# Queries, keys, values and gate of a head group as one product of seven half-size products

## The reference

```
q, k, v = xn @ Wq.T, xn @ Wk.T, xn @ Wv.T          # 32 query heads, 8 key/value heads of 128
q, k = rmsnorm(q) * q_norm_w, rmsnorm(k) * k_norm_w
a = softmax(q k^T / sqrt(128) + slope[h] * (key - query), causal) @ v
s = a @ Wo.T
g = silu(xn @ W.T + bias + sum_n 2 lora_weights[n] * (xn @ A_n.T) @ B_n.T)
x + s * g
```

## Time and profile before

| | us |
|---|---|
| median of 3 runs (2854.84 to 2856.85) | 2855.52 |
| the profiled execution | 2851.0 |
| its span, first to last instruction | 2849.2 |
| PE busy, weight loads busy | 2763.9, 2516.4 |
| DVE, ACT, POOL busy | 2198.6, 1259.9, 1136.4 |
| q1, the queue of SP | 237.35 MB, 25.2% of the engines' time |

### The profile page before, as it was taken

The page is one execution under the profiler, slowest core; times in us unless marked ns, Lnnn a source line. Parts: engine busy times, 40 slices in busy tenths (PEclk is TensorE's granted clock), DMA queues, the critical chain, the costliest instruction groups (busy, mean ns, idle before and its releaser), DMA issues.

```text
span 2849.2 us, 47788 instructions
## 1 busy us (share of the span) xinstructions
PE 2763.9 (97%) x18256; PEld 2516.4 (88%) x18256; DVE 2198.6 (77%) x5317; ACT 1259.9 (44%) x2907; POOL 1136.4 (40%) x555
## 2 busy tenths in 40 slices
PE   7999999998999999999899999999989999999997
PEld 6899999997889999999688999999878999999985
DVE  6877777778787777777878777777787877777788
ACT  3444444444344444444434444444443444444443
POOL 3334334333434434334353334443344433344334
PEclk9999999999999999999999999999999999999999
DMA  7222222212422221221341222222224222222213
GB/s 256 97 79 67 65 70 64 64 61 96 168 66 86 75 67 60 68 75 57 106 168 52 72 75 75 67 69 65 71 96 160 67 61 66 75 75 68 74 62 113
DMA packets 80659, 240.40 MB, mean 84 GB/s; under 512 B 9008, under 2 KB 17328, under 8 KB 79920
## 3 DMA queue, kind: packets, MB, share of 16 engines
q1 hardware_dynamic: 80432, 237.35, 25.2%
HBM read 217.39 MB, written 19.92 MB: 83 GB/s over the span
## 4 chain that ended last, share of the span: by engine, by line
PE 83%; DVE 14%; issue 2%; ACT 0%; DMA 0%; SPq 0%; POOL 0%; POOLq 0%; DVEq 0%; ACTq 0%
PE proj L402 20%; PE proj L403 20%; PE proj L404 20%; PE tr L472 4%; PE sc L402 3%; PE ot L403 3%; PE ot L404 3%; PE sc L404 3%; PE sc L403 3%; DVE g_buf L1155 3%; PE ot L402 3%; PE tr L484 2%; DVE sq L1060 2%; DVE prob L1126 1%; DVE xtok L1050 1%
## 5 line engine op out<-in xcount | busy, mean ns | idle before, releaser
L916 POOL TENSOR_TENSOR wb_lo<-stage_b,wb_hi 128x1024 fp32r<-128x1024 f32 x158 | 382.3, 2419 | 1424.6 <-ACT wb_hi L684 1424.6
L402 PE MATMUL proj<-wa_hi,xn_hi 128*128 128x256 f32 x3072 | 878.3, 286 | 0.9 <-issue 0.9
L404 PE MATMUL proj<-wa_hi,xn_lo 128*128 128x256 f32 x3072 | 869.3, 283 | 0.0
L403 PE MATMUL proj<-wa_lo,xn_hi 128*128 128x256 f32 x3072 | 869.2, 283 | 0.0
L402 PEld LDWEIGHTS proj<-wa_hi,xn_hi 128*128 128x128 f32 x3072 | 589.0, 192 | 2.5 <-issue 2.1
L403 PEld LDWEIGHTS proj<-wa_lo,xn_hi 128*128 128x128 f32 x3072 | 589.3, 192 | 0.3
L404 PEld LDWEIGHTS proj<-wa_hi,xn_lo 128*128 128x128 f32 x3072 | 588.9, 192 | 0.0
L911 POOL TENSOR_TENSOR wa_lo<-stage_a,wa_hi 128x1024 fp32r<-128x1024 f32 x192 | 463.1, 2433 | 228.7 <-ACT wa_hi L670 228.7
L709 ACT ACTIVATE prob<-prob,negmax 128x128 f32<-128x128 f32 (+3 forms) x512 | 286.5, 560 | 431.0 <-DVE negmax L1116 430.1
L402 PE MATMUL proj<-o_hi,wb_hi 128*128 128x512 f32 x1024 | 431.5, 421 | 41.7 <-DVE acc L1143 40.3
L1143 DVE TENSOR_TENSOR acc<-acc,proj 128x512 f32<-128x512 f32 x480 | 326.9, 682 | 116.0 <-PE proj L404 113.3
(11 more groups left out here) (120 smaller groups left out, 4778.9 us busy)
## 6 DMA issues: line engine op xcount, KB each, us to landing
stage_a<-wa SPq DMA_DIRECT2D x196, 512.0 KB, 3.6
stage_b<-wo SPq DMA_DIRECT2D x128, 512.0 KB, 3.7
stage_b<-weff SPq DMA_DIRECT2D x30, 512.0 KB, 3.8
xtok<-x_tok SPq DMA_DIRECT2D x4, 2048.0 KB, 8.6
outT<-acc SPq DMA_DIRECT2D x32, 256.0 KB, 2.0
gate_dram<-x_buf SPq DMA_DIRECT2D x28, 256.0 KB, 2.2
xtok<-xT SPq DMA_DIRECT2D x16, 256.0 KB, 4.1
xtok<-gate_dram SPq DMA_DIRECT2D x16, 256.0 KB, 4.7
```

Of the source, the lines that this page charges most:

```text
L402: pe.matmul(out, hi_l, hi_r, start=first, stop=False)
L403: pe.matmul(out, hi_l, lo_r, start=False, stop=False)
L404: return pe.matmul(out, lo_l, hi_r, start=False, stop=last)
L916: pool.tensor_tensor(wb_lo[:, slot, :], stage_b[:, slot, :], wb_hi[:, slot, :], ALU.subtract).then_inc(wb_ready, 1)
```

## The change

The 512 tokens by 1024 of xn are seen as 2x2 blocks (token halves, width halves), and the 1024x896 weights of a group (q0, q1, k, half the gate, then q2, q3, v, the other half of the gate) as 2x2 blocks of 512x448. Their product is made with seven products of half size (Strassen's scheme in Winograd's form) instead of eight: P1 and P2 of plain blocks, P6, P7, P4, P5, P3 with one or both sides a sum of blocks.

- **Weight sums.** For each of 8 groups, once, the seven 512x448 operands are made and stored to DRAM (`wu`, two halves each): three plain blocks by `store_halves`, four sums by `store_sums`, after `weight_sums` on VectorE (half 0) and GpSimd (half 1). Group 0's and 1's are made in the opening, group n+2's during group n (n = 0 to 5). Wo is copied once from DRAM to DRAM (`copy_b`) and loaded from there.
- **Token sums.** `x_sum` makes four of them in place on GpSimd; seven operands of 4 chunks are turned and split in 14 fills a batch, spread over steps (6,3) to (7,2).
- **Pieces.** `piece(n, p, t)`: 128 of the half's 256 tokens, 4 chunks, three matmuls of 448 columns each. P2, P7 and P3 go on in the bank that holds P1, P6 and P5, after that has been read. `UNIT` puts P1, P2 into step 0, P6, P7 into 1, P4 into 2, P5, P3 into 3 of the group before. ScalarE copies P1 and P1+P2 out; VectorE adds the others to rows of `raw` (`take_piece`), ten a group.
- **Gate.** Its 128 columns of group n come out with the group's rows, are turned (four transposes), and finished in the same group; there is no gate product of its own.
- **Uniform groups.** All 32 groups are the same code written out, with constants in place of registers; the pieces of the next batch's group 0 are made in group 7, and each batch's result is finished in steps 1 and 2 of the next batch's group 0, in two halves that share four slots of `xtok`.
- **Squares** are taken by ScalarE with an accumulator (`squares`, 20 a group), the value's low half by GpSimd. Weights are loaded into the buffer of their low part and split there; there are four half slots.

```
-KV, Q01, Q23 = 0, 1, 2
-
-PROJ = [[(Q23, t) for t in range(4)],
-        [(KV, 0), (KV, 1), (KV, 2)],
-        [(KV, 3), (Q01, 0), (Q01, 1)],
-        [(Q01, 2), (Q01, 3)]]
...
+HALF = 448
...
+NP = 7
+HW = 2 * NP
+P1, P2, P6, P7, P4, P5, P3 = range(NP)
+UNIT = [(P1, P2), (P6, P7), (P4,), (P5, P3)]
+FRESH = (P1, P6, P4, P5)
+CHAINED = {P2: P1, P7: P6, P3: P5}
...
+            def store_halves(g, h):
+                sp.wait_ge(prep_in[h], 192 * (g + 1))
+                for p, a, c in ((P1, 0, 0), (P2, 1, 0), (P3, 1, 1)):
+                    sp.dma_start(wu[(g * NP + p) * 2 + h].rearrange("p (k n) -> p k n", k=2),
+                                 prep_tile(g, h, a, c)).then_inc(prep_bst[h], 16)
+
+            def store_sums(g, h):
+                sp.wait_ge(prep_t[h], 4 * (g + 1))
+                for p, a, c in ((P6, 1, 1), (P7, 0, 1), (P4, 1, 0), (P5, 0, 0)):
+                    sp.dma_start(wu[(g * NP + p) * 2 + h].rearrange("p (k n) -> p k n", k=2),
+                                 prep_tile(g, h, a, c)).then_inc(prep_tst[h], 16)
...
+                load_b(4 * n + j - 1)
+                copy_b(4 * n + j + 1)
+                if j == 0:
+                    if g == 0 and b > 0:
+                        load_result(b - 1, 0)
+                    if new is not None:
+                        sp.wait_ge(prep_tst[1], 64 * new)
+                        load_weights(new, 0)
+                        load_gate_weights(new, 0)
+                    load_product(n + 1, P6)
+                    if new is not None:
+                        store_halves(new, 0)
+                    load_product(n + 1, P7)
+                if j == 1:
+                    if new is not None:
+                        store_sums(new, 0)
+                    load_product(n + 1, P4)
+                    if new is not None:
+                        sp.wait_ge(prep_tst[0], 64 * (new + 1))
+                        load_weights(new, 1)
+                        load_gate_weights(new, 1)
+                    load_product(n + 1, P5)
+                    if new is not None:
+                        store_halves(new, 1)
+                    if g == 0 and b > 0:
+                        store_result(b - 1, 0)
+                if j == 2:
+                    if g == 0 and b > 0:
+                        load_result(b - 1, 1)
+                    load_product(n + 1, P3)
+                    if new is not None:
+                        store_sums(new, 1)
+                if j == 3:
+                    load_product(n + 2, P1)
+                    load_product(n + 2, P2)
...
+            def piece(n, p, t):
+                if p in FRESH:
+                    bank = proj_bank(("u", n, p, t))
+                else:
+                    bank = proj_ps[PJ["u", n, CHAINED[p], t] % 2]
+                    if p == P2:
+                        pe.wait_ge(u_act, u_act_count(n, P1, t))
+                    else:
+                        pe.wait_ge(u_dve, u_dve_count(n, CHAINED[p], t))
...
+                for h in range(2):
+                    w = HW * n + 2 * p + h
+                    if t == 0:
+                        pe.wait_ge(w_ready, w + 1)
+                    for i in range(2):
+                        k = 2 * h + i
+                        mm = three(bank[:, 0:HALF], xh[:, p, k, tok], xl[:, p, k, tok],
+                                   wh[:, w % 4, i, :], wl[:, w % 4, i, :],
+                                   p in FRESH and k == 0, k == 3, p in CHAINED)
+                    if h == 0 and t == 1:
+                        mm.then_inc(w_half, 1)
+                mm.then_inc(u_done, 1)
...
+                pieces, fills = unit_pieces(n, j), x_fills(n, j)
+                while len(fills) > len(pieces):
+                    turn_x(fills.pop(0))
+                for u in pieces:
+                    piece(*u)
+                    if fills:
+                        turn_x(fills.pop(0))
+                if v >= 0:
+                    out_ready(v)
+                    out_proj(v, 0)
+                    out_proj(v, 1)
+                pe.wait_ge(prob_ready, m + 1)
+                turn_probs(m, (0, 1, 2))
+                if v >= 0:
+                    out_proj(v, 2)
+                turn_probs(m, (3,))
+                if v >= 0:
+                    out_proj(v, 3)
...
+                for i, head in enumerate(heads):
+                    at = (("q0", "q1", "k", "q2", "q3").index(head)) * 4 + row
+                    ins = act.activation(junk[:, turn % 2, i, :], raw[:, row, COL[head]:COL[head] + HD],
+                                         ACT.Square, accum_out=ss[:, at:at + 1])
...
+                for k in range(3):
+                    probs_hi(m, k)
+                split_product(*[(n + 1, P6), (n + 1, P4), (n + 1, P3), (n + 2, P1)][j])
+                probs_hi(m, 3)
+                if j != 2:
+                    split_product(*[(n + 1, P7), (n + 1, P5), None, (n + 2, P2)][j])
...
+                pool.wait_ge(w_hi_done, w + 1)
+                pool.tensor_tensor(w_slot(wl, w), w_slot(wl, w, True), w_slot(wh, w), ALU.subtract
+                                   ).then_inc(w_ready, 1)
...
+                bias_of(m + 1)
+                low_b(v + 1)
+                if j == 0:
+                    values_lo(n)
+                low_product(*[(n + 1, P6), (n + 1, P4), (n + 1, P3), (n + 2, P1)][j])
...
+                if j != 2:
+                    low_product(*[(n + 1, P7), (n + 1, P5), None, (n + 2, P2)][j])
...
+                if j == 2 and n + 2 < HKV:
+                    weight_sums(n + 2)
...
+                dst, src = {P6: (raw[:, t, right], raw[:, t + 2, left]),
+                            P7: (raw[:, t + 2, right], raw[:, t + 2, left]),
+                            P4: (raw[:, t + 2, left], raw[:, t + 2, right]),
+                            P5: (raw[:, t + 2, right], raw[:, t + 2, right]),
+                            P3: (raw[:, t, right], raw[:, t, right])}[p]
+                dve.wait_ge(u_done, u_count(n, p, t))
+                dve.tensor_tensor(dst, src, bank, ALU.add).then_inc(u_dve, 1)
...
+                normalise(m)
+                if m > 0:
+                    head_out(m - 1)
+                if j == 0:
+                    queries_lo(n, 1)
+                if j == 1:
+                    queries_lo(n, 2)
+                    queries_lo(n, 3)
+                if j == 3 and more:
+                    keys_lo(n + 1)
+                    queries_lo(n + 1, 0)
+                pieces, fills = unit_pieces(n, j), x_fills(n, j)
...
+                for u in pieces:
+                    p, t = u[1:]
+                    if p not in (P1, P2):
+                        take_piece(*u)
...
+                add_out(v, 0)
+                if j == 2 and more:
+                    row_factors(n + 1, 0)
+                add_out(v, 1)
+                for k in range(3):
+                    probs_lo(m, k)
+                if j == 2 and more:
+                    scale_rows("k")
+                if j == 1:
+                    gate_product(n)
+                add_out(v, 2)
+                probs_lo(m, 3)
+                add_out(v, 3)
+                if j == 0 and n + 2 < HKV:
+                    weight_sums(n + 2, 0)
```

More of the change, by code:

```diff
@@ new lines, in turn_gate, with turn_probs @@
+            def turn_gate(n):
+                pe.wait_ge(u_dve, u_dve_count(n, P3, 1))
+                turn_rows(("z", n), COL["gate"])
+            def turn_probs(m, key_tiles):
+                for k in key_tiles:
+                    bank = turn_bank(("p", m, k))
+                    for i in range(k, NT):
+                        a = P_AT[i] + k * P
+                        mm = pe.transpose(bank[:, i * P:i * P + P], prob[:, a:a + P], ident_sb[:])
+                    mm.then_inc(tr_done, 1)
@@ L653, in _, with out_ready, out_proj @@
-            batch(0, True)
-            for b in range(1, BATCH):
-                batch(b, False)
+            def out_ready(v):
+                pe.wait_ge(wb_ready, v + 1)
+                pe.wait_ge(ot_free, v // 2 * 2 + 2)
+            def out_proj(v, c):
+                bank = proj_bank(("o", v, c))
+                pair = v % 4 // 2
+                for hh in range(2):
+                    w = slice(hh * 512 + c * P, hh * 512 + c * P + P)
+                    mm = three(bank[:], wb_hi[:, v % 2, w], wb_lo[:, v % 2, w],
+                               o_hi[:, pair, hh, :], o_lo[:, pair, hh, :], hh == 0, hh == 1)
+                mm.then_inc(out_done, 1)
@@ new lines, in rsqrt, with take_hi @@
+            def rsqrt(n, part):
+                at, chain = [slice(0, 12), slice(12, 20)][part], 2 * n + part
+                act.wait_ge(sq_done, 4 * chain + 4)
+                act.activation(lnv[:, at], ss[:, at], ACT.Ln, bias=eps_sb[:, 0:1]).then_inc(ln_done, 1)
+                act.wait_ge(ln_done, chain + 1)
+                act.activation(rinv[:, at], lnv[:, at], ACT.Exp, scale=-0.5).then_inc(r0_done, 1)
```

(37 more changed lines are left out.)

1772 lines of the change are left out of this document (781 added, 991 removed).

## The result

The changed kernel takes 3101.64 us (median; 3094.95 to 3111.77) against 2855.91 of the kernel before in the same comparison: 1.086 times as long, interval 1.083 to 1.089. Forecast were 2782 us and a range of 2700 to 2875; rival 3, the shared port, was on the right side, at 2875.

A forecast was written before the change was run, and what follows sets the result against it. TensorE was taken to bound the middle, waits the edges. Opening 128, 31 groups of 78.2, stall 62, preparation 54, batch edges, remaining products and end gave 2774 us of span, 2782 as time; range 2700 to 2875.

The forecast's parts named there:

- rival 3: Shared port: VectorE's SBUF instructions wait for GpSimd's, 5 instead of 2 us a group, 2875 us; chance 0.16.
- The products: TensorE: 168 matmuls of 448 columns a group, 0.2005 us apart, 1078 us in all for 1281, saving 203.
- Rival 4: A 448-column matmul costs what a 512-column one does: 148 us more, 2930; chance 0.03.
- 62 us of stall: TensorE waiting for VectorE's takes of banks by order inside a step: 2.0 us a group, 31 groups.
- the walk of the steps: Timing inside steps: normalising at 7.6 us, VectorE at the bank 10.3 to 10.9, TensorE wanting it at 9.7.
- the prediction's own signs of being wrong: Later batches' mid groups over 84 us, four normalising instructions averaging 2 us or more, or opening over 160.
- Preparation, 9 us a group: Making weight sets behind groups 0 to 5: 9 us for each of 6 groups (0 to 20), 54 in all.
- The other suspect: Wo tile queued behind stored sums, landing late; ScalarE stands still before the probability halves: 6 us of TensorE.
- Rival 2: Preparation binds through the single queue's in-order waits: 20 us for each of six groups, 2848; chance 0.11.
- The opening: Before the first scores: a chain of loads, merge, stores and sums; first scores at about 128 us (105 to 160).
- A batch's end, 11 us with the turns: Change of batch: some 7 us of token turns plus 4 us a boundary (0 to 15) for VectorE, three times.
- The end: Last group +12 us without covering pieces, then two output tiles, and results 16 us behind the last matmul.

The follow-up runs named there:

- a_shortlow: Changed kernel with GpSimd's low part of the weights made on only 32 of 896 columns; 2859.54 us, 1.001 of the kernel before.
- a_normact: Changed kernel with the four normalising instructions moved from VectorE to ScalarE; 2971.97 us, 1.042 of the kernel before.
- b_moved: All the work of a_normact in another order, sums, scalings and results put behind takes, loads and stores moved along; 2839.24 us, 0.995 of the kernel before.
- d_keys: b_moved with the opening's loads and sums reordered and the keys' row scaling moved between step 3's score maxima; 2794.41 us, 0.9795 of the kernel before.

## Why the prediction was wrong

- **The products** were right. The forecast had a start every 0.2005 us at 448 columns; TensorE in order of time in a middle group of the changed kernel shows 0.207 (0.203 in other stretches), over 5376 matmuls 35 us at most, and a group without gaps takes 78.8 us against 78.2. Rival 4 is out.

```profile
1390.68 0.37 PE L461 MATMUL proj<-wh,xh 128*128 128x448 f32 x1
1390.88 0.37 PE L462 MATMUL proj<-wl,xh 128*128 128x448 f32 x1
1391.09 0.37 PE L463 MATMUL proj<-wh,xl 128*128 128x448 f32 x1
```

- **"62 us of stall", of which the port none.** The step that failed first, 150 us of 319. The prediction had the mechanism as rival 3, with the place (the normalising ahead of the banks' takes) and a threshold of 4.4 us a group over 78.2; it measured 7.0 (6.4 over the 78.8 of a_shortlow). What argued it down was that additions out of a bank don't show the port. They don't (609 ns after), but they queue behind instructions that do. And the rows had both prices for the four, 1.27 in the earlier trace rows and 3.85 in the earlier trace rows; the walk of the steps used the small one although it had placed GpSimd's low parts at the same moment. It also left out the clock, which in a middle group adds 0 to 2.4 us to the two waits. The place was right in part: the waits are in step 1 (P6) and step 2 (P4), while in step 3, where both the walk and the rival had set P5's, normalising took 1.3 us and TensorE did not wait. The rival's own 5 us a group was 2 short of the 7.0 measured over the forecast's 78.2, 62 us in 31 groups; the rest of the way from 2875 to 3102 is the other terms. Two of the prediction's own signs of being wrong came out: middle groups over 84 us, and four normalising instructions of 3.5 us together on average for its limit of 2.
- **Preparation, 9 us a group.** Group 1 to 5 paid 15 each, 77 for 45. The price of VectorE's four sums ("delay the scores of step 1 by up to 6") measured 9.4 as a single wait; in a_normact, where the same wait is 9.39 us, three of the four sums met GpSimd, and the clock was at its lower level behind it. The other suspect is there too, ScalarE standing idle for the Wo tile, but no long wait of TensorE is owed to it. ScalarE's row over the whole changed kernel, and TensorE's waits from 443 to 543 us, one such group:

```profile
L690 ACT ACTIVATE wb_hi<-wb_lo 128x1024 fp32r<-128x1024 f32 x128 | 135.1, 1055 | 93.6 <-DMA wb_lo<-wo_in 93.6
```

```profile
PE sc L461 <- DVE negmax L1070: 9.4, 1, 9.4
PE proj L461 <- DVE raw L1065: 7.6, 2, 5.5
```

  b_moved shows that little of it was the amount: 2.9 us a group in another order, and some 8 more once, in group 6, with the same bytes through the same queue. Rival 2's "preparation binds" is true of the time (96 to 116 us for six sets) and false of the cause it named.
- **Group 0.** The opening came out to the microsecond (127.6 for 128), with some luck, since the first product began at 65.3 us for a forecast 61; its consequence was missed: 38 us. The prediction stopped at the first scores; the second weight set was still in the queue, and P1 of group 1 waited 25.9 us for it. TensorE's waits from 122 to 240 us, changed kernel:

```profile
PE proj L461 <- POOL wl L867: 25.9, 1, 25.9
PE sc L461 <- DVE negmax L1070: 14.4, 3, 10.5
```

- **A batch's end, 11 us with the turns.** It cost 35 to 43. The work was listed (statistics, scaling, results) and priced by TensorE's turns plus 4 us "for VectorE". In a_normact all three intervals still cost 9 to 14, with one to four waits of over 1 us each and the lower clock behind some of them; two of the three went to 0.5 and 3.6 us when the work was put behind takes. On the port it is dearer still: 7.9, 18.6 and 8.8 us over a middle group in the changed kernel's second batch.
- **The end**, 18 us short, was not taken apart.

The forecast was of the right work and of an order it had not checked. Each edge was priced at its cost when nothing meets; with work moved away from where it met, middle groups of 79.3 us and 2794 us in all came out, though the ends of a batch and group 0 stayed dearer than forecast.

## What to carry to other kernels

An instruction that shares a port costs its own time or the other engine's whole instruction. When a change adds work to that other engine, take every instruction of the first that reads SBUF alone and stands ahead of something the bound engine waits for, and price it at the long time. Work that nobody needs yet (sums for a later group, statistics, results) belongs behind the first instruction that frees a buffer, one piece at a time, never as a block at a step's end; here that, with the loads and stores moved along, was worth 118 us with nothing left out. And look at the granted clock behind each wait of the tensor engine: where it falls the wait costs more than its length, here about 1 us for each fall.

## What was not expected of the hardware

- The port's price goes by GpSimd's instruction and not by its busy time: cut in four, its work took longer (1224 against 992 us in all) and the kernel ran 87 us faster.
- The waits of TensorE of 1.8 to 2.1 us, which look harmless in a span of 3000, were followed by some 3 us at the lower clock in 19 of 32 cases in the middle groups, and in 13 by none: groups 9, 10 and 11, with the same two waits, last 83.7, 86.3 and 84.7 us. The kernel before, at 97% busy, hardly had it; the mean granted clock was 0.99 before, 0.94 after and 0.98 in d_keys.
- ScalarE normalised with a scale per partition at 395 to 713 ns for 128 to 512 columns, 2.2 us for the four against VectorE's 1.28 alone, and was still the better place.
